# RWKV attention and a mixture of experts on one core: the combination of the experts' outputs moved from a stage of its own into the block loop

## The chip, the cores and the metric

The kernel runs on one core of a Trainium2 chip. The metric is the device time of one execution, in microseconds (us). A core has five engines with queues of their own: TensorE (PE), VectorE (DVE), ScalarE (ACT), GpSimd (POOL) and SyncE (SP). They are ordered only by semaphores, and each engine takes its own instructions in order, so an instruction that waits holds up everything queued behind it on that engine.

## The reference, cut to what matters

The input x is (2, 2048, 256), in float32. Two layers follow each other, each with a residual and a layer norm:

```python
x = layernorm(x + attn(x))     # RWKV: a scan over time, gates, projections
x = layernorm(x + ffn(x))      # mixture of 8 experts, the best 2 for each token

logits = x @ Wg + bg
scores, idx = top_k(logits, 2); scores = softmax(scores)
h = tokens @ W1[e] + b1[e]     # 256 -> 1024, for each expert e
a = gelu(h) for even e, silu(h) for odd e
y = a @ W2[e] + b2[e]          # 1024 -> 256
out = sum over the 2 chosen experts of score * y
```

There are 4096 tokens and so 8192 pairs of a token and an expert. The kernel computes y only for the chosen pairs.

## The kernel before

**Attention stage.** Eight chunks of 512 tokens (256 of each batch). `chunks(step)` writes the order of the work out by hand for each engine, as a software pipeline. In step i VectorE runs `stabilise(i)` (scans o_all, then nd), `divide(i-1)`, `place(i-3)`, `accumulate(i)` (b2v, two long scans), `numerator(i)`, `statistics(i-1)`, `choose(i-2)` and `lower_halves(i+2)`. ScalarE's step is `exponents(i)` (two Relu, two Exp, of which B is the first), `bonuses(i)`, a copy, `gates(i+1)` (Sigmoid), `upper_halves(i+2)` (which waits for TensorE's transposes xT), `inverse(i)` (Ln, Exp), `normalise_x1(i-1)` and the copies `copy_v(i+1)`. `accumulate` waits for the Exp of B, and TensorE makes the transposes of chunk i+2 in the order of its own step, behind the projection that waits for nd of chunk i. `choose` finds each token's two experts, `place` gives each pair a row in its expert's region of records_dram, and POOL's `send_records` scatters each token's row twice with indirect DMAs. A record is x1 (256 numbers), the pair's label and one slot number.

**Block stage.** The regions are cut into blocks of 256 rows with one expert each. At most 41 blocks can be used, here 35; the first two (`EARLY`, expert 0) run before the counts of all experts are known. A small table in SBUF holds each block's first row, expert and more. For each block t:

- ScalarE loads the records, `load_records(t+3)`, and runs `activate_block(t+1)`: for four groups b, two activations from hT_ps with bias (L1074) and a rounded copy aTh (L1080). A table load stands ahead of the first activation of a block.
- TensorE transposes the records of t+2, makes the first product of t+1 (hT_ps, L869) and the second of t (y_ps, L878, in two halves h). Each operand is held as an upper and a lower part, three products each.
- VectorE runs `outputs(t-1)` (y_sb = y_ps + bias, L1200), `halves(t+2)` and `lower_parts(t+1)` (aTl = hT_ps - aTh, L1192).
- POOL scatters y_sb to expert_out_dram, `scatter(t)`, two indirect DMAs a block (L670), and at the start of each expert splits the weights of the expert two ahead into upper and lower part, `split(e)` (L576, L580). SyncE loads those weights into one buffer, `raw`, once the split before is done.

Records live in 4 buffers (`RING`). The wait that releases the load of a block's records in ScalarE's `block_step` is on dest_done, which VectorE sets in `halves`, early:

```python
u = t + 3
if u.exists:
    with if_used(act, used, u):
        after(act, dest_done, (u - RING).upto(BH))
        load_records(u)
u = t + 1
if u.exists:
    with if_used(act, used, u):
        activate_block(u)
```

VectorE, ScalarE and POOL run the blocks 4 to 31 in hardware loops of four, TensorE all blocks in line. `if_used` puts a branch around blocks from 32 on.

**Combination stage.** When all scatters have landed (a wait of SyncE), 16 pieces of 128 tokens of each batch are taken: SyncE loads both outputs of each token (yy), VectorE adds score * first output to x1 (L1470), ScalarE scales the second (L1122), VectorE adds it (L1478) and makes statistics (L1484, L1492), POOL makes rstd (L686 to L691), ScalarE normalises (L1135), SyncE stores.

## Time and profile before

| | us |
|---|---|
| median of 3 runs (lowest, highest) | 736.69 (736.32, 737.68) |
| the profiled execution, its own time | 733.24 |
| its span, from the first to the last instruction | 731.5 |
| TensorE busy | 636.5 (87%) |
| VectorE busy | 457.7 (63%) |
| ScalarE busy | 392.8 (54%) |
| POOL busy | 304.9 (42%) |
| TensorE's granted clock, mean | 0.922 of full |

Busy times are of the one profiled execution. The instructions of an engine are named by line, operation and the program's tile names with buffer numbers left out; an arrow and a name in brackets behind a row is what ended the idle time before it. Busy time of PE is modelled from pipelined matmuls. Instructions that load a register, branch or wait are not counted as busy; they appear with a q behind the engine's name.

### The profile page before, as it was taken

The numbers are of one execution on the slowest core, as the hardware profiler recorded it, in microseconds if no ns is written. First come the engines' busy times: TensorE is split into PE (matmuls) and PEld (weight loads), VectorE is DVE, ScalarE is ACT, GpSimd is POOL, SyncE is SP. The second block draws the span as 40 slices with busy tenths as digits, with TensorE's granted clock in tenths as the row PEclk, the third lists the DMA queues.
The fourth block names the chain that finished last, engine by engine and source line by source line (L and its number), as shares of the span: only waits on it lengthen the run. The fifth ranks groups of instructions, "written<-read, shape, count | busy, mean of one in ns | idle before, by whom it ended". The sixth has DMA issues, their size and how long they took to land.

```text
span 731.5 us, 14706 instructions
## 1 busy us (share of the span) xinstructions
PE 636.5 (87%) x4472; PEld 595.0 (81%) x4472; DVE 457.7 (63%) x963; ACT 392.8 (54%) x715; POOL 304.9 (42%) x353
## 2 busy tenths in 40 slices
PE   5999999999957599999999999999999999997000
PEld 4887878878746499999999999999999999996000
DVE  3769999999994575574554654455444444432694
ACT  3566586577651263645545464655636364542474
POOL 5111044644655557282371641551921722122363
PEclk9999999999975599999999999999999999999555
DMA  8400232322226436905142141141141112101893
GB/s 254 137 29 1 87 101 82 107 91 83 88 87 231 144 101 223 330 28 175 44 136 70 44 160 52 42 161 46 49 154 38 39 46 59 32 27 32 276 304 117
DMA packets 57116, 78.75 MB, mean 108 GB/s; under 512 B 5190, under 2 KB 46611, under 8 KB 56884
## 3 DMA queue, kind: packets, MB, share of 16 engines
q1 hardware_dynamic: 41540, 51.59, 21.8%
q0 software_dynamic: 6496, 16.99, 6.5%
q10 hardware_dynamic: 8976, 8.72, 4.3%
q8 instruction: 73, 1.20, 0.7%
q14 instruction: 31, 0.25, 0.1%
HBM read 49.14 MB, written 28.92 MB: 107 GB/s over the span
## 4 chain that ended last, share of the span: by engine, by line
PE 67%; DVE 16%; issue 7%; ACT 3%; POOL 2%; DMA 2%; SPq 0%; ACTq 0%; DVEq 0%; POOLq 0%
PE hT_ps L869 27%; PE y_ps L878 26%; PE vr_ps L722 4%; PE k_ps L722 4%; PE xT_ps L887 2%; PE wo_ps L730 2%; DVE o_all L1214 2%; PE small_ps L744 1%; DVE stats L1312 1%; DVE newton L1237 1%; DVE newton L1235 1%; DVE newton L1242 1%; POOL rstd_c L689 1%; DVE num L1304 1%; DVE num L1307 1%
## 5 line engine op out<-in xcount | busy, mean ns | idle before, releaser
L869 PE MATMUL hT_ps<-xTh,wx 128*128 128x256 f32 x1120 | 211.3, 287 | 0.7 <-issue 0.6
L878 PE MATMUL y_ps<-wx,aTh 128*128 128x256 f32 x1088 | 197.5, 283 | 0.9 <-DVE y_sb L1200 0.9
L869 PEld LDWEIGHTS hT_ps<-xTh,wx 128*128 128x128 f32 x1120 | 178.2, 193 | 1.0 <-issue 0.9
L878 PEld LDWEIGHTS y_ps<-wx,aTh 128*128 128x128 f32 x1088 | 169.7, 192 | 1.1 <-issue 1.1
L1192 DVE TENSOR_TENSOR aTl<-hT_ps,aTh 128x512 fp32r<-128x512 f32 x140 | 93.1, 688 | 119.2 <-ACT aTh L1080 119.2
L670 POOL DMA_INDIRECT expert_out_dram<-y_sb,dest x70 | 68.3, 976 | 238.0 <-DVE y_sb L1200 222.3
L869 PE MATMUL hT_ps<-xTl,wx 128*128 128x256 f32 x560 | 159.2, 284 | 0.0
L878 PE MATMUL y_ps<-wx,aTl 128*128 128x256 f32 x544 | 154.0, 283 | 0.0
L1074 ACT ACT_TABLE_LOAD x33 | 42.3, 1283 | 170.4 <-PE hT_ps L869 165.2
L1074 ACT ACTIVATE hT_ps<-hT_ps,b_c 128x256 f32<-128x256 f32 x280 | 113.8, 469 | 18.2 <-DVE dest L1182 14.8
L869 PEld LDWEIGHTS hT_ps<-xTl,wx 128*128 128x128 f32 x560 | 108.3, 193 | 0.0
L878 PEld LDWEIGHTS y_ps<-wx,aTl 128*128 128x128 f32 x544 | 104.4, 192 | 0.0
L635 POOL DMA_INDIRECT records_dram<-rec,slot_i x64 | 75.2, 1175 | 63.4 <-DVE rec L1338 33.9
L722 PE MATMUL vr_ps<-xh,wq 128*128 128x512 f32 x256 | 87.5, 414 | 0.0
L1080 ACT ACTIVATE aTh<-hT_ps 128x512 fp32r<-128x512 f32 x140 | 84.2, 647 | 0.0
L1200 DVE TENSOR_TENSOR y_sb<-y_ps,b_b 128x256 f32<-128x256 f32 x70 | 29.3, 424 | 79.6 <-PE y_ps L878 77.7
L580 POOL TENSOR_TENSOR wx<-staging,wx 128x512 fp32r<-128x512 f32 x56 | 70.4, 1300 | 0.6
L722 PEld LDWEIGHTS vr_ps<-xh,wq 128*128 128x128 f32 x256 | 50.3, 196 | 11.7
L722 PE MATMUL vr_ps<-xl,wq 128*128 128x512 f32 x128 | 52.1, 407 | 0.0
L722 PE MATMUL k_ps<-xh,wq 128*128 128x512 f32 x128 | 44.1, 417 | 4.4 <-DVE nd L1221 2.3
L730 PE MATMUL wo_ps<-wo,newton 128*128 128x256 f32 x128 | 36.4, 435 | 7.5 <-DVE newton L1242 3.8
L730 PEld LDWEIGHTS wo_ps<-wo,newton 128*128 128x128 f32 x128 | 27.4, 217 | 13.1 <-issue 4.2
(194 smaller groups left out, 855.2 us busy)
## 6 DMA issues: line engine op xcount, KB each, us to landing
staging<-in_L_ffn_W SPq DMA_DIRECT2D x16, 1024.0 KB, 8.5
recs<-records_dram ACTq DMA_DIRECT2D x33, 258.0 KB, 2.7
yy<-expert_out_dram SPq DMA_DIRECT2D x16, 512.0 KB, 5.5
xin<-in_L_attn_x SPq DMA_DIRECT2D x16, 256.0 KB, 4.3
xres<-in_L_attn_x SPq DMA_DIRECT2D x16, 256.0 KB, 3.0
x_dram<-rec SPq DMA_DIRECT2D x16, 256.0 KB, 3.4
xx<-x_dram SPq DMA_DIRECT2D x2, 2048.0 KB, 20.2
out<-res SPq DMA_DIRECT2D x16, 256.0 KB, 3.7
```

The lines of the kernel that those rows point to most:

```text
L580: pool.tensor_tensor(wx[:, e % 2, 1, at], raw[:, at], wx[:, e % 2, 0, at].bitcast(F32), ALU.subtract).then_inc(weights_ready if n == LOWER ...
L635: pool.indirect_dma_start(xs, bass.IndirectOffsetOnAxis(ap=slot_i[at][:, n:n + 1], axis=0), rec[at][:, j, :], None, bounds_check=DUMMY - 1 ...
L670: pool.indirect_dma_start(ys, bass.IndirectOffsetOnAxis(ap=dest[t.slot][:, h:h + 1], axis=0), y_sb[t.slot][:, h, :], None, bounds_check=2 ...
L722: ins = pe.matmul(out_ps.rearrange("p (b t) -> p b t", b=B), wq[:, mat, now, part, cc, oc * P:(oc + 1) * P], xpart[c.slot][:, cc, :, now:n ...
L730: ins = pe.matmul(wo_ps[:, h, :], mixed[:, cc, b, h * P:(h + 1) * P], wo[:, cc, :], start=cc == 0, stop=cc == CC - 1)
L869: ins = pe.matmul(hT_ps[b][:, f, :], wx[:, s, part, off:off + P], xpart[t.slot % 2][:, cc, :], start=k == 0, stop=k == len(terms) - 1)
L878: ins = pe.matmul(y_ps[h], apart[t.slot % 2][:, fc, h * P:(h + 1) * P], wx[:, s, part, off:off + C], start=k == 0, stop=k == len(terms) - 1)
L887: ins = pe.transpose(xT2_ps[:, cc, h * P:(h + 1) * P], recs[u.slot][:, h, cc * P:(cc + 1) * P], ident[:])
L1074: act.activation(hT_ps[b][:, f, :], hT_ps[b][:, f, :], func, bias=b1_c[:, bass.ds(expert * FC + (2 * b + f), 1)]).then_inc(act_done, 1)
L1080: act.activation(aTh[u.slot % 2][:, 2 * b - 2:2 * b, :], hT_ps[b - 1][:], ACT.Copy).then_inc(aTh_done, 1)
L1192: dve.tensor_tensor(aTl[u.slot % 2][:, 2 * b:2 * b + 2, :], hT_ps[b][:], aTh[u.slot % 2][:, 2 * b:2 * b + 2, :].bitcast(F32), ALU.subtract ...
L1200: dve.tensor_tensor(y_sb[u.slot][:, h, :], y_ps[h], b2_b[:, bass.ds(expert * C, C)], ALU.add).then_inc(y_done, 1)
```

## The change

The combination stage is gone. A record has five numbers beside x1 instead of two: the token, the slot of its best expert, the larger of its two slots, and its two weights. VectorE's `mark` finds for each row of a block whether its token's other share is still to come or already there. Two times weight * (y + b2) is added to x1, which makes a *share*; the two shares of a token add up to twice the row before the layer norm (hence 4 * EPS). The first share of a token is scattered over its row of x1_dram (`keep_shares`); the block with the second share gathers the first (`gather`), adds, makes statistics, normalises and scatters the finished rows to the output (`send_rows`). The weights are split by ScalarE (upper part) and VectorE (lower part) in four pieces each, at the first block of the expert before. ScalarE loads records for t+4 at the end of its step and waits for the shares of t ahead of it. All engines run the blocks in line. The scores are two Sigmoids of ScalarE in the attention stage (`weigh`). The diff, cut to its core:

```diff
+            def weigh(c):
+
+                at = c.number % RECS
+                act.wait_ge(gap_done, c.upto(1))
+                scattered(act, c)
+                act.activation(rec[at][:, :, C + 3], gap[:], ACT.Sigmoid, scale=-1.0).then_inc(weighed, 1)
+                act.activation(rec[at][:, :, C + 4], gap[:], ACT.Sigmoid).then_inc(weighed, 1)
...
+                if (i - 3).exists and i.number < NCH:
+                    weigh(i - 3)
                 if i.exists:
...
                     inverse(i)
+                if i.number == NCH:
+                    weigh(i - 2)
                 if (i - 1).exists:
                     normalise_x1(i - 1)
+                if i.number in (NCH - 1, NCH + 1):
+                    weigh(i - 2)
...
+            rows_1 = x1d.rearrange("b t c -> (b t) c")
+            rows_2 = out.rearrange("b t c -> (b t) c")
+
+            def spread_z(t):
+                pool.wait_ge(mv_z_done, since_second(t) * BH)
+                after(pool, row_done, since_second(t - RING) * BH)
+                pool.tensor_tensor(var_z[:], mv_z[t.slot][:, :, 1], eps4_b[:], ALU.add).then_inc(var_done, 1)
+                pool.wait_ge(var_done, since_second(t))
+                pool.tensor_tensor(rstd_z[t.slot][:], var_z[:], half_neg[:, 0:BH], ALU.pow).then_inc(rstd_z_done, 1)
+
+            def keep_shares(t):
+
+                pool.wait_ge(marks, t.upto(8))
+                pool.wait_ge(share_done, t.upto(BH))
+                take_wait(pool)
+                for h in range(BH):
+                    pool.indirect_dma_start(
+                        rows_1, bass.IndirectOffsetOnAxis(ap=where_to[t.number % MARKS][:, 0, h:h + 1], axis=0),
+                        share[t.slot][:, h, :], None, bounds_check=TOKENS - 1, oob_is_err=False).then_inc(share_out[t.slot], 16)
+
+            def gather(t):
+
+                pool.wait_ge(marks, t.upto(8))
+                pool.wait_ge(share_out[(t - 1).slot], (t - 1).turn(16 * BH, 16 * BH))
+                after(pool, sum_done, since_second(t - RING))
+                take_wait(pool)
+                for h in range(BH):
+                    pool.indirect_dma_start(
+                        other[t.slot][:, h, :], None, rows_1,
+                        bass.IndirectOffsetOnAxis(ap=where_to[t.number % MARKS][:, 1, h:h + 1], axis=0),
+                        bounds_check=TOKENS - 1, oob_is_err=False).then_inc(other_in[t.slot], 16)
+
+            def send_rows(t):
+                pool.wait_ge(row_done, since_second(t) * BH)
+                take_wait(pool)
+                for h in range(BH):
+                    pool.indirect_dma_start(
+                        rows_2, bass.IndirectOffsetOnAxis(ap=where_to[t.number % MARKS][:, 1, h:h + 1], axis=0),
+                        row_out[t.slot][:, h, :], None, bounds_check=TOKENS - 1, oob_is_err=False).then_inc(out_done[t.slot], 16)
+
+            keep_shares(early_block(0))
+
+            def block_step(t):
+                for stage, u in ((keep_shares, t - 1), (send_rows, t - 2), (gather, t), (spread_z, t - 1)):
+                    if stage is keep_shares:
+
+                        if t.exists:
+                            with if_used(pool, used, t, t.number - 1):
+                                stage(u)
+                    elif u.exists and with_second(u):
+                        with if_used(pool, used, u, t.number - 1):
+                            stage(u)
+
+            blocks_in_line(pool, used, 2, block_step)
...
+                slot = pe.value_load(par_t[0:1, bass.ds(t.number, 1)], min_val=0, max_val=1)
+                full = pe.value_load(full_t[0:1, bass.ds(t.number, 1)], min_val=0, max_val=1)
+                pe.wait_ge(aTl_done, t.upto(FC // 2))
+                pe.wait_ge(share_done, (t - 1).upto(BH, 1))
+                with pe.If(slot == 0):
+                    product2(t, 0, 0)
+                with pe.Else():
+                    product2(t, 1, 0)
+                pe.wait_ge(share_done, (t - 1).upto(BH))
...
+            def split_upper(t):
+
+
+                kind = act.value_load(split_t[0:1, bass.ds(t.number, 1)], min_val=0, max_val=2)
+                with act.If(kind > 0):
+                    expert = act.value_load(next_t[0:1, bass.ds(t.number, 1)], min_val=0, max_val=E - 1)
+                    slot = act.value_load(opp_t[0:1, bass.ds(t.number, 1)], min_val=0, max_val=1)
+                    for h in range(BH):
+                        act.wait_ge(mm2_done[h], (t - 1).upto(1))
...
+                    act.wait_ge(raw_in, expert * 32 + 64)
+                    take_wait(act)
+                    for n in range(SPLITS):
+                        at = bass.ds(n * WE // SPLITS, WE // SPLITS)
+                        act.activation(wx[:, bass.ds(slot, 1), 0, at].rearrange("p a b -> p (a b)"), raw[:, at], ACT.Copy).then_inc(hi_done, 1)
...
-            act.wait_ge(dest_done, early_block(0).upto(BH))
+            act.wait_ge(share_done, early_block(0).upto(BH))
             load_records(early_block(4))
             activate_block(early_block(2))
+            act.wait_ge(share_done, early_block(1).upto(BH))
+            load_records(early_block(5))
             used = blocks_in_use(act)
 
             def block_step(t):
-                u = t + 3
-                if u.exists:
-                    with if_used(act, used, u):
-                        after(act, dest_done, (u - RING).upto(BH))
-                        load_records(u)
                 u = t + 1
                 if u.exists:
                     with if_used(act, used, u):
                         activate_block(u)
...
+                if t.number == EARLY:
+                    act.wait_ge(split_known, 1)
+                split_upper(t)
+                u = t + RING
+                if u.exists:
+                    with if_used(act, used, u):
+                        act.wait_ge(share_done, t.upto(BH))
+                        load_records(u)
+
+            blocks_in_line(act, used, 0, block_step)
...
+            def mark(u, own):
+
+
+                n = u.slot % 2
+                rows = recs[u.slot]
+                dve.tensor_tensor(is_top[n][:], rows[:, :, C + 1], own, ALU.is_equal).then_inc(marks, 1)
+                dve.tensor_tensor(is_late[n][:], rows[:, :, C + 2], own, ALU.is_equal).then_inc(marks, 1)
+                dve.tensor_tensor(is_early[n][:], rows[:, :, C + 2], own, ALU.not_equal).then_inc(marks, 1)
+                dve.tensor_tensor(lead[n][:], rows[:, :, C + 3], rows[:, :, C + 4], ALU.subtract).then_inc(marks, 1)
...
+                dve.wait_ge(marks, u.upto(8, 2))
+                dve.scalar_tensor_tensor(out=where_to[u.number % MARKS][:, 0, :], in0=is_late[n][:], scalar=float(NOWHERE),
+                                         in1=rows[:, :, C], op0=ALU.mult, op1=ALU.add).then_inc(marks, 1)
+                dve.wait_ge(marks, u.upto(8, 3))
+                dve.scalar_tensor_tensor(out=where_to[u.number % MARKS][:, 1, :], in0=is_early[n][:], scalar=float(NOWHERE),
+                                         in1=rows[:, :, C], op0=ALU.mult, op1=ALU.add).then_inc(marks, 1)
+                dve.wait_ge(marks, u.upto(8, 4))
+                dve.scalar_tensor_tensor(out=twice[n][:], in0=is_top[n][:], scalar=2.0, in1=lead[n][:],
+                                         op0=ALU.mult, op1=ALU.mult).then_inc(marks, 1)
+                dve.wait_ge(marks, u.upto(8, 7))
+                dve.scalar_tensor_tensor(out=weight[u.slot][:], in0=rows[:, :, C + 4], scalar=2.0, in1=twice[n][:],
+                                         op0=ALU.mult, op1=ALU.add).then_inc(marks, 1)
...
+            def share_half(u, h, expert):
+
+                if h == 0:
+                    after(dve, share_out[u.slot], u.turn(16 * BH))
+                    after(dve, sum_done, since_second(u - RING))
+                    dve.wait_ge(marks, u.upto(8))
+                dve.wait_ge(mm2_done[h], u.upto(1))
+                dve.tensor_tensor(y_ps[h], y_ps[h], b2_b[:, bass.ds(expert * C, C)], ALU.add).then_inc(y_done, 1)
+                dve.wait_ge(y_done, u.upto(BH, h + 1))
+                dve.scalar_tensor_tensor(out=share[u.slot][:, h, :], in0=y_ps[h], scalar=weight[u.slot][:, h:h + 1],
+                                         in1=recs[u.slot][:, h, 0:C], op0=ALU.mult, op1=ALU.add).then_inc(share_done, 1)
+
+            def shares(u):
+                expert = dve.value_load(ex_t[0:1, bass.ds(u.number, 1)], min_val=0, max_val=E - 1)
                 for h in range(BH):
-                    dve.wait_ge(mm2_done[h], u.upto(1))
-                    dve.tensor_tensor(y_sb[u.slot][:, h, :], y_ps[h], b2_b[:, bass.ds(expert * C, C)],
-                                      ALU.add).then_inc(y_done, 1)
+                    share_half(u, h, expert)
+
+            def add_other(u):
+                dve.wait_ge(other_in[u.slot], in_ring(u) * 16 * BH)
+                after(dve, out_done[u.slot], (in_ring(u) - 1) * 16 * BH)
+                dve.wait_ge(share_done, u.upto(BH))
+                dve.tensor_tensor(row_out[u.slot][:], share[u.slot][:], other[u.slot][:], ALU.add).then_inc(sum_done, 1)
+                dve.wait_ge(sum_done, since_second(u))
+                for h in range(BH):
+                    dve.bn_stats(stats_z[u.slot][:, h, :], row_out[u.slot][:, h, :]).then_inc(bn_z, 1)
+                dve.wait_ge(bn_z, since_second(u) * BH)
+                take_wait(dve)
+                for h in range(BH):
+                    dve.bn_aggr(mv_z[u.slot][:, h, :], stats_z[u.slot][:, h, :]).then_inc(mv_z_done, 1)
+
+            def normalise(u):
+                dve.wait_ge(rstd_z_done, since_second(u))
+                for h in range(BH):
+                    dve.tensor_scalar(row_out[u.slot][:, h, :], row_out[u.slot][:, h, :], mv_z[u.slot][:, h, 0:1],
+                                      rstd_z[u.slot][:, h:h + 1], ALU.subtract, ALU.mult).then_inc(row_done, 1)
...
+                kind = dve.value_load(split_t[0:1, bass.ds(t.number, 1)], min_val=0, max_val=2)
+                with dve.If(kind > 0):
+                    expert = dve.value_load(next_t[0:1, bass.ds(t.number, 1)], min_val=0, max_val=E - 1)
+                    slot = dve.value_load(opp_t[0:1, bass.ds(t.number, 1)], min_val=0, max_val=1)
...
+                        dve.wait_ge(hi_done, expert * SPLITS + (n + 1))
+                        take_wait(dve)
+                        flat = lambda part: wx[:, bass.ds(slot, 1), part, at].rearrange("p a b -> p (a b)")
+                        dve.tensor_tensor(flat(1), raw[:, at], flat(0).bitcast(F32),
+                                          ALU.subtract).then_inc(weights_ready if n == SPLITS - 1 else lower_done, 1)
...
+                u = t - 1
+                if u.exists and with_second(u):
+                    with if_used(dve, used, u, known):
+                        add_other(u)
+                if t.exists:
+                    with if_used(dve, used, t, known):
+                        shares(t)
+                        if t.number == EARLY:
+                            split_steps()
+                            dve.wait_ge(split_known, 1)
+                        split_lower(t)
+
+            blocks_in_line(dve, used, 2, block_step)
```

`split_steps` is twelve small operations on VectorE (up to 128x246), each waiting for the one before, that fill the tables split_t, next_t and opp_t; ScalarE waits for them once, at t = 2.

## Rows read from the trace of the kernel before

**Rows 1.** The page's part 4, the chain that ended last, shares of the span by line.

```profile
PE hT_ps L869 27%; PE y_ps L878 26%; PE vr_ps L722 4%; PE k_ps L722 4%; PE xT_ps L887 2%; PE wo_ps L730 2%; DVE o_all L1214 2%; PE small_ps L744 1%; DVE stats L1312 1%; DVE newton L1237 1%; DVE newton L1235 1%; DVE newton L1242 1%; POOL rstd_c L689 1%; DVE num L1304 1%; DVE num L1307 1%
```

**Rows 2.** Windows: start:end, length; busy us (x instructions) by engine, PEclk, DMA share, GB/s.

```profile
95.00:120.00 25.00, 24.59 (x121) 20.27 (x120) 24.27 (x56) 16.70 (x24) 13.17 (x15) 0.93 0.32 107
300.00:400.00 100.00, 100.00 (x839) 100.00 (x838) 54.78 (x85) 52.12 (x107) 44.96 (x36) 1.00 0.36 117
680.00:690.00 10.00, 0.00 (x0) 0.00 (x0) 7.59 (x22) 4.75 (x11) 3.46 (x8) 0.50 0.92 323
```

**Rows 3.** VectorE's timeline, end of the block stage: start us, length us, instruction [idle before].

```profile
672.41 0.42 DVE L1200 TENSOR_TENSOR y_sb<-y_ps,b_b 128x256 f32<-128x256 f32 x1 [2.27 <-PE y_ps L878]
```

**Rows 4.** The chain in order of time, block stage: start us, us, what.

```profile
300.88 5.75 PE hT_ps L869 x48
...
312.82 5.75 PE hT_ps L869 x48
```

**Rows 5.** ScalarE's timeline, block stage.

```profile
292.10 1.28 ACT L1074 ACT_TABLE_LOAD   x1 [1.61 <-PE hT_ps L869]
...
314.36 1.28 ACT L1074 ACT_TABLE_LOAD   x1 [5.66 <-PE hT_ps L869]
```

**Rows 6.** ScalarE's timeline, attention stage.

```profile
91.19 0.21 ACT L1008 ACTIVATE xh<-xh 128x4 fp32r<-128x4 f32 x1 [4.27 <-PE xT_ps L713]
...
92.39 1.28 ACT L1017 ACT_TABLE_LOAD   x1
...
94.77 1.28 ACT L1019 ACT_TABLE_LOAD   x1
...
101.85 1.05 ACT L981 ACTIVATE B<-B 128x1024 f32<-128x1024 f32 x1
...
116.91 0.21 ACT L1008 ACTIVATE xh<-xh 128x4 fp32r<-128x4 f32 x1 [4.75 <-PE xT_ps L713]
...
202.87 1.05 ACT L981 ACTIVATE B<-B 128x1024 f32<-128x1024 f32 x1
```

**Rows 7.** VectorE's timeline, attention stage.

```profile
96.47 1.38 DVE L1221 SCALAR_TENSOR_TENSOR nd<-o_all,consts_c,k_ps 128x512 f32<-128x512 f32 x2
...
102.93 1.23 DVE L1276 TENSOR_TENSOR b2v<-B,v 128x1024 f32<-128x1024 f32 x1
...
204.99 1.22 DVE L1276 TENSOR_TENSOR b2v<-B,v 128x1024 f32<-128x1024 f32 x1
```

**Rows 8.** VectorE's groups by line: instruction, xcount | busy us, mean ns | idle before.

```profile
L1470 DVE SCALAR_TENSOR_TENSOR zz<-yy,score,xx 128x256 f32<-128x256 f32 x32 | 13.7, 468 | 9.1 <-DMA yy<-expert_out_dram 9.0
L1484 DVE BATCH_NORM_STATS2 stats_c<-zz 128x6 f32<-128x256 f32 x32 | 11.9, 411 | 0.0
...
L1478 DVE TENSOR_TENSOR zz<-zz,y 128x512 f32<-128x512 f32 x16 | 10.9, 682 | 3.8 <-ACT y L1122 3.7
...
L1304 DVE TENSOR_TENSOR num<-bonus,p_all 128x1024 f32<-128x1024 f32 x8 | 9.9, 1233 | 0.3
...
L1492 DVE BATCH_NORM_AGGREGATE mv_c<-stats_c 128x2 f32<-128x6 f32 x32 | 3.9, 161 | 0.2 <-DVE stats_c L1484 0.2
```

**Rows 9.** ScalarE's queue at L1065, 289 to 293 us: xcount: ns, first to last start.

```profile
L1065 ACTq TENSOR_LOAD <-row_t x1: 282/282/282, 290.2 to 290.2; - x1
```

**Rows 10.** VectorE's timeline, block stage.

```profile
297.92 1.29 DVE L1192 TENSOR_TENSOR aTl<-hT_ps,aTh 128x512 fp32r<-128x512 f32 x2 [0.52 <-ACT aTh L1080]
```

**Rows 11.** VectorE's queue at L1448: xcount: ns min/median/max, first to last start.

```profile
L1448 DVEq TENSOR_LOAD <-ex_t x34: 300/305/319, 291.4 to 666.0; - x34
```

**Rows 12.** POOL's groups by line, columns as in rows 8.

```profile
L670 POOL DMA_INDIRECT expert_out_dram<-y_sb,dest x70 | 68.3, 976 | 238.0 <-DVE y_sb L1200 222.3 <-issue 14.9
...
L689 POOL TENSOR_TENSOR rstd_c<-var_e,half_neg 128x2 f32<-128x2 f32 x16 | 11.1, 696 | 1.3
```

**Rows 13.** DMA issues: xcount, median us from issue to landing.

```profile
expert_out_dram<-y_sb,dest POOLq DMA_INDIRECT x70, 2.9
```

**Rows 14.** POOL's timeline, attention stage.

```profile
209.51 1.88 POOL L635 DMA_INDIRECT records_dram<-rec,slot_i  x1 [0.30 <-issue]
```

383 lines of the change are left out of this document (142 added, 241 removed).

## The prediction

> **What bounds the kernel now.** I read the page's chain of waits first: two lines of TensorE, hT_ps (27%) and y_ps (26%), make half of it [rows 1]. The windows then show three stages. Up to about 255 us runs the attention stage, where VectorE is busy 24.3 of 25 us. From there to 672.8 us runs the block stage, with TensorE busy 100 of 100 us, VectorE only 55 and ScalarE 52. Behind 672.8 us TensorE does nothing (0.00 us): the combination takes 731.5 - 672.8 = 58.7 us of the span [rows 2, 3]. The chain in order of time gives the period of a block: 312.82 - 300.88 = 11.94 us, which is two products of 5.75 us and four transposes [rows 4]. 35 blocks are used, two of them early. ScalarE idles 5.66 us in each period until TensorE's first product is there [rows 5]. So the question is not whether the 58.7 us can go, but whether the block stage stays at 11.94 us when the combination's work is laid into it. S(t) below is the moment when both shares of block t are done.
>
> **The attention stage: +8.0.** Each chunk gets two Sigmoids on 128x4 in `weigh`, ahead of `exponents`, for chunks 3 to 7. ScalarE's table then has to go from Exp to Sigmoid and back: two loads of 1.28 and about 0.25 for the two small operations, 2.8 us. (Bounds for one chunk: 0 if both loads fell into idle time, 1.5 if Sigmoid's table also had Exp; no gain is possible, nothing is taken out of ScalarE's chain.) Is it hidden? ScalarE starts when the transposes xT are there (91.19) and runs without idle to the end of B's Exp at 101.85 + 1.05 = 102.90; VectorE starts b2v at 102.93 [rows 6, 7]. No slack at all: chunk 3 pays 2.8. Chunk 4 pays nothing more, because ScalarE's start at 116.91 hangs on TensorE's transposes, which follow nd of chunk 3 (done at 97.85) by 19 us, and that has not moved; chunk 5 pays 2.8 again, 6 nothing. In chunk 7 B is ready at 203.92 and b2v starts at 204.99: 1.1 of slack, 1.7 paid. Sum 7.3. One more operation of 128x4 in `place` adds some 0.09 to the full VectorE in 8 chunks: 0.7. The scores' three steps go from the table (1 us), but VectorE waits for ScalarE behind them, so nothing is gained.
>
> A rule of the Trainium skill (ScalarE: Activation LUTs, "What ACT_TABLE_LOAD costs") puts a switch of tables at 1.28 us of load and a drain of 1.38, 2.66 together. The trace does not show the drain: the load at 92.39 ends at 93.67 and the next load row (94.77) follows one operation of 1.06 without a gap [rows 6]. With the rule a chunk would pay 5.6 and the stage 5.6 + 5.6 + 4.5 + 0.7 = 16.4.
>
> **Into the block stage: +0.4.** The split of expert 1's weights leaves POOL; ScalarE's four copies (about 1 us each) lie in time in which it waits for the pad rows. VectorE gets four subtractions of 128x1024 at 1.23 [rows 8] between `halves` of blocks 2 and 3, and the marks; by its sum (four times 1.16, two halves of 1.4, two marks of 1.1, shares of 1.8) its first lower part of block 2 is done some 0.4 after TensorE wants it. Expert 1's weights stay in time. POOL's clearing of `other`, the records' 12 more bytes a row, and the longer unrolled code cost nothing by this: nobody waits for them early. Their cost if that is wrong: a microsecond or two, once.
>
> **The block stage: a new loop.** TensorE's own waits are harmless: share_done(t-1) is asked for behind a first product of 5.75 us. What matters is `block_step` of ScalarE. It ran `load_records(t+3)` on dest_done, a mark long set. Now it waits for share_done(t), and only behind that come load_records(t+4) and then activate_block(t+2), queued on the same engine. VectorE's step t+1 does lower_parts(t+2), which need those activations, then add_other(t), then shares(t+1). So S(t) releases ScalarE, ScalarE releases VectorE, and VectorE makes S(t+1): a loop of one block in which TensorE has no part. Its length:
> - ScalarE from the wait to its table load: the load of the row number starts at 290.2, the table load at 292.10 with the DMA issue and the expert's number between them; with the semaphore 2.0 [rows 5, 9].
> - Table load to the end of VectorE's last lower part: 297.92 + 1.29 - 292.10 = 7.1 [rows 5, 10].
> - add_other: 128x512 addition 0.69, two statistics 0.74, a wait of 0.16, two aggregates of which the second starts 0.08 later: 1.75 [rows 8].
> - the expert's number behind it: the load alone is 0.31 [rows 11], with the register work that follows it 0.65, as ScalarE's is 0.5 out of its 2.0. It may be hidden (0) or cost 1.0 with the branches; now VectorE reads it while a long operation still runs, here the one ahead is 0.16 long, so I take it whole.
> - two halves of shares: addition 0.42 [rows 3], the multiply-add 0.47 [rows 8], the second half overlapping a little: 1.65 to 1.8, taken 1.65.
>
> Sum 2.0 + 7.1 + 1.75 + 0.65 + 1.65 = 13.15 us, against 11.94. Bounds: 12.1 with every doubtful term at its least, 14.0 at its most. Marks (eight small operations), halves and `normalise` lie in VectorE's wait for the activations.
>
> **The sum.** S(2) is 301.8: the product ends near 300.9, plus 0.9. `split_steps` (12 small operations; 1.9 at 0.16 each, 5.6 at 0.47, taken 3.7) come next, and ScalarE waits for them: 305.5. Then 0.6 for the split's kind, 2.0, 7.1 and 1.75 give S(3) = 317.0. From there to S(30) are 27 turns: 355.0. Six of them hold a split of weights. ScalarE's four copies end just as the share comes; VectorE's part, four times 1.16 and the numbers it reads, pushes its next lower parts behind the activations by about 2.5 (0 if it caught up, 5 if nothing overlapped): 15. S(30) = 687.0. From t = 31 ScalarE's wait lies in a branch not taken (block t+4 is unused), and TensorE and VectorE finish the last four blocks in turn: with S(30) as zero, S(31) is 13.15, the product of block 32 starts on the first share at 12.3 and ends at 18.1, the first product of 34 at 24.2, the product of 33 at 30.0; its share lets the last product start at 30.4, and S(34) is 37.1. S(34) = 724.1, where now it is 672.8.
>
> **The tail: 58.7 becomes 16.** The combination's stage goes whole: SyncE's wait for all scatters, the loads back, 32 sums, the statistics, POOL's and ScalarE's part, the stores. What comes in its place is each block's own, and only the last two blocks' stand behind the end. Behind S(34): POOL sends block 32's rows, gathers, spreads block 33, then 34 in turn; an indirect DMA is 0.98 with 0.30 before it, the power 0.69, the last landing 2.9 [rows 12, 13]. keep 3.2, send 2.6, gather 2.6, its landing and the addition 4.5, spread, normalise and send 34: end 16 behind S(34), 13 to 20 with the branches.
>
> Span: 724.1 + 16 + 8.0 = 748.1, that is +16.6 on 731.5 (the 0.4 is in S(2)). The profiled execution took 733.24 us with 1.74 around its span, so it would read 749.8. The median of the runs is 736.69; +16.6 gives 753.3.
>
> **Rivals.**
> - *TensorE stays the bound (faster).* If the loop is no longer than 11.94, S(34) stays at 672 and the end is 672 + 0.4 + 16 + 8.0 = 696.8, time 702. For it: VectorE's and ScalarE's busy sums are far under the period, and the value loads may hide. Against: the chain is serial, and its largest parts (7.1, 2.0) stand in the trace whole. Between 11.94 and 13.15 it goes by 27 us for each microsecond; no change is at a loop of 12.5.
> - *POOL becomes the bound (slower still).* Six indirect DMAs a block instead of two. At 1.28 each it has 7.7 of 13.15. But a row of before shows 1.88 with 0.30 ahead of it, while VectorE ran a long scan [rows 14]. Six at 2.18 and a spread of 1.2 are 14.3: 1.1 more a block, some 31 us, 784. It decides from 2.0 each. The Trainium skill (SBUF — State Buffer, the box on the "DVE blocks DMA" trap) says that GpSimd can't write descriptors while VectorE holds the shared port; the change gives VectorE more such operations. The slow row agrees with it, but most of the 70 rows at 976 ns ran beside VectorE too.
> - *The attention stage pays nothing*: -8.0, 745; against it stands the slack of 0.03 us.
> - *The table's drain exists*, as a mechanism of the five chunks: +8.4, 762. The gapless rows speak against.
> - That the change doesn't do what it says: the records are loaded four blocks ahead in name, but released later than now in time. This is the forecast itself.
>
> **How the numbers follow.** Forecast 0.60 (its own range 735 to 772); a short loop, 702 to 735, 0.22; POOL 0.07; attention free 0.06; drain 0.05. A measurement of this kernel can tell 0.2% (1.5 us) from no change. Faster 0.22, within 0.2% 0.02, slower 0.76. The loop's bounds of 12.1 and 14.0 give 725 and 776; with the other terms I take 720 to 778.
>
> **What would show it.** In the changed profile: ScalarE's idle time ahead of its table load or row load released by VectorE's shares, not by TensorE; a period near 13.15 between first products; TensorE idle about 1.2 us a block in two gaps; the first table load behind copy_v in chunks 3 to 7 and a wait of b2v for B. A period of 11.94 with idle ScalarE would make the forecast wrong, and so would shares that end long before ScalarE asks.

## The result: 774.5 us, 5.0% slower

The changed kernel takes 774.47 us (median of 4 runs, 773.57 to 776.31) beside 737.18 us for the kernel before: a ratio of 1.050 [1.049, 1.052]. The forecast was 753.3: slower, and the time lies in the outer range of 720 to 778, but above the 735 to 772 of the main case; +16.6 us stood where +37.3 were measured. The profiled execution took 776.31 us, its span is 774.4 (731.5 before). The two profiled executions lie 42.9 us apart in span and the medians 37.3, because the one of before was 3.9 us under its median and this one 1.8 over; the stages below add up to the 42.9.

The page's parts on the chain and the clock. PEclk is TensorE's granted clock in tenths, in 40 slices:

```profile
PEclk9999999999855699998999998999999999899995
DVE 31%; PE 23%; issue 19%; ACT 12%; ACTq 5%; DVEq 3%; another core or an unknown queue 1%; DMA 1%; POOL 1%; SPq 1%; POOLq 0%
```

Before, two lines of TensorE alone made half of the chain [rows 1]. Now VectorE leads it, and ScalarE, VectorE and their register loads (ACTq, DVEq) make half. Two windows of [rows 2] again. Columns: window, its length, busy us of PE, PEld, DVE, ACT, POOL, then PEclk, DMA share and GB/s. TensorE is no longer full in the block stage, and its clock is under 1.00 there:

```profile
95.00:120.00 25.00, 23.80 (x123) 19.27 (x122) 21.42 (x44) 18.99 (x28) 11.49 (x13) 1.00 0.33 107
300.00:400.00 100.00, 93.49 (x760) 91.61 (x759) 65.55 (x177) 53.72 (x105) 38.59 (x42) 0.97 0.26 80
```

One turn of the loop, VectorE's side. Columns: start, duration, engine and line, in brackets the idle time before and its releaser:

```profile
487.69 0.42 DVE L1210 TENSOR_TENSOR y_ps<-y_ps,b_b 128x256 f32<-128x256 f32 x1
488.14 0.48 DVE L1212 SCALAR_TENSOR_TENSOR share<-y_ps,weight,recs 128x256 f32<-128x256 f32 x1
...
494.11 0.69 DVE L1195 TENSOR_TENSOR aTl<-hT_ps,aTh 128x512 fp32r<-128x512 f32 x1 [2.13 <-ACT aTh L1063]
...
496.53 1.29 DVE L1195 TENSOR_TENSOR aTl<-hT_ps,aTh 128x512 fp32r<-128x512 f32 x2 [0.52 <-ACT aTh L1063]
497.74 0.68 DVE L1224 TENSOR_TENSOR row_out<-share,other 128x512 f32<-128x512 f32 x1
498.45 0.75 DVE L1227 BATCH_NORM_STATS2 stats_z<-row_out 128x6 f32<-128x256 f32 x2
499.34 0.25 DVE L1231 BATCH_NORM_AGGREGATE mv_z<-stats_z 128x2 f32<-128x6 f32 x2
500.30 0.43 DVE L1210 TENSOR_TENSOR y_ps<-y_ps,b_b 128x256 f32<-128x256 f32 x1 [0.71 <-issue]
...
501.63 0.48 DVE L1212 SCALAR_TENSOR_TENSOR share<-y_ps,weight,recs 128x256 f32<-128x256 f32 x1
```

And ScalarE's side of the same turn, its record load and then its table load:

```profile
489.34 0.39 ACTq L1049 DMA_DIRECT2D recs<-records_dram  x1
490.62 1.28 ACT L1057 ACT_TABLE_LOAD   x1 [7.24 <-issue]
```

The shares of block 14 end at 488.62. ScalarE, idle for 7.24 us with nothing of TensorE to wait for (it idled 5.66 for TensorE in [rows 5]), asks for the records 0.72 later and loads its table at 490.62. The chain in order of time goes there too, from the share to ScalarE's load of the row number (L1048):

```profile
488.14 0.49 DVE share L1212
488.66 0.28 ACTq L1048
```

VectorE's last lower part ends at 497.82, add_other at 499.59, the row of the number takes 0.71, and the shares of block 15 end at 502.11. 2.00 + 7.20 + 1.77 + 0.71 + 1.81 = 13.49 us, forecast as 2.0 + 7.1 + 1.75 + 0.65 + 1.65 = 13.15. It is the loop that was forecast, and it sets the period: the turns without a split take 13.39 to 13.77 us.

Where the 42.9 us of span came from. S(t) is again the end of both shares of block t, read from the rows of L1212:

| stretch | forecast | after | difference |
|---|---|---|---|
| up to S(2) | 309.8 (301.8 + 8.0) | 316.9 | +7.1 |
| S(2) to S(3), with split_steps | 15.2 | 15.5 | +0.3 |
| S(3) to S(30), 27 turns, 6 with a split | 370.0 | 379.3 | +9.3 |
| S(30) to S(34) | 37.1 | 43.9 | +6.8 |
| S(34) to the end of the span | 16 | 18.9 | +2.9 |
| span (the rows are rounded) | 748.1 | 774.4 | +26.3 |

### The profile page after: what moved, and what is told of

It reads as the page before. It is cut to its first block, busy times and chain, and to the rows that moved or that the text cites. A ratio compares the mean times of both kernels' runs of the same rounds, so it can differ in the third digit from the quotient of the medians.

```text
span 774.4 us, 14695 instructions
## 1 busy us (share of the span) xinstructions
PE 657.0 (85%) x4472; PEld 604.4 (78%) x4472; DVE 552.1 (71%) x1398; ACT 411.8 (53%) x709; POOL 349.1 (45%) x422
## 4 chain that ended last, share of the span: by engine, by line
DVE 31%; PE 23%; issue 19%; ACT 12%; ACTq 5%; DVEq 3%; another core or an unknown queue 1%; DMA 1%; POOL 1%; SPq 1%; POOLq 0%
DVE aTl L1195 6%; ACT hT_ps L1057 5%; PE vr_ps L697 5%; PE hT_ps L844 5%; PE k_ps L697 4%; PE y_ps L853 3%; DVE share L1212 3%; DVE y_ps L1210 3%; DVE stats_z L1227 3%; DVE wx L1514 2%; ACT aTh L1063 2%; PE wo_ps L705 2%; DVE row_out L1224 2%; PE small_ps L719 2%; ACTq L1049 1%
## 5 line engine op out<-in xcount | busy, mean ns | idle before, releaser
L844 PE MATMUL hT_ps<-xTh,wx 128*128 128x256 f32 x1120 | 224.4, 298 | 16.2 <-DVE aTl L1195 15.5
L844 PEld LDWEIGHTS hT_ps<-xTh,wx 128*128 128x128 f32 x1120 | 188.6, 204 | 21.9 <-DVE aTl L1195 20.8
L853 PEld LDWEIGHTS y_ps<-wx,aTh 128*128 128x128 f32 x1088 | 167.0, 189 | 17.5 <-issue 17.5
L844 PE MATMUL hT_ps<-xTl,wx 128*128 128x256 f32 x560 | 165.1, 295 | 0.0
L1057 ACT ACTIVATE hT_ps<-hT_ps,b_c 128x256 f32<-128x256 f32 x280 | 113.4, 468 | 22.2 <-PE hT_ps L844 15.6
L631 POOL DMA_INDIRECT x_dram<-share,where_to x68 | 72.9, 1072 | 104.9 <-issue 96.1
L844 PEld LDWEIGHTS hT_ps<-xTl,wx 128*128 128x128 f32 x560 | 114.4, 204 | 0.0
L590 POOL DMA_INDIRECT records_dram<-rec,slot_i x64 | 76.5, 1196 | 65.7 <-DVE rec L1375 34.9
L651 POOL DMA_INDIRECT out<-row_out,where_to x64 | 62.8, 981 | 75.6 <-DVE row_out L1236 53.3
L642 POOL DMA_INDIRECT other<-x_dram,where_to x64 | 65.9, 1030 | 25.0 <-issue 24.7
L1210 DVE TENSOR_TENSOR y_ps<-y_ps,b_b 128x256 f32<-128x256 f32 x70 | 29.9, 428 | 28.3 <-issue 22.4
```

What stands on the lines that cost most here:

```text
L590: pool.indirect_dma_start(xs, bass.IndirectOffsetOnAxis(ap=slot_i[at][:, n:n + 1], axis=0), rec[at][:, j, :], None, bounds_check=DUMMY - 1 ...
L631: pool.indirect_dma_start(rows_1, bass.IndirectOffsetOnAxis(ap=where_to[t.number % MARKS][:, 0, h:h + 1], axis=0), share[t.slot][:, h, :], ...
L642: pool.indirect_dma_start(other[t.slot][:, h, :], None, rows_1, bass.IndirectOffsetOnAxis(ap=where_to[t.number % MARKS][:, 1, h:h + 1], ax ...
L651: pool.indirect_dma_start(rows_2, bass.IndirectOffsetOnAxis(ap=where_to[t.number % MARKS][:, 1, h:h + 1], axis=0), row_out[t.slot][:, h, : ...
L844: ins = pe.matmul(hT_ps[b][:, f, :], wx[:, s, part, off:off + P], xpart[t.slot % 2][:, cc, :], start=k == 0, stop=k == len(terms) - 1)
L853: ins = pe.matmul(y_ps[h], apart[t.slot % 2][:, fc, h * P:(h + 1) * P], wx[:, s, part, off:off + C], start=k == 0, stop=k == len(terms) - 1)
```

## Experiments

Ratios are to the kernel before on the same chip; the changed kernel's is 1.050. Where a stage is meant and not the whole, S(2) and S(3) to S(30) of the profiled execution stand beside the time, because chips and executions differ in the early part by more than some effects do.

**The two orders.** First, add_other behind the shares, everything else as in the change:

```
-   add_other(t - 1)
    shares(t)
+   add_other(t - 1)
    split_lower(t)
```

> Only VectorE's order in a step changes: add_other(t-1) behind shares(t). The records are still loaded four ahead behind share(t). Theory of the loop: 1.77 us of it go, and a part of the 0.71 us of the number read, which now lies behind a longer operation; 11.2 to 11.7 is under TensorE's 11.94, so 27 turns give back 42 us, and the end some 3 to 7 more because the last product waits less for VectorE: 725 to 732 us if the splits keep their 2.45 us, 715 if they hide. Rival (the sum of VectorE's work, which is unchanged, sets the period): no change.

718.04 us, ratio 0.981 [0.979, 0.984]. Most turns take 11.04 to 11.42 in place of 13.5 (three early ones up to 11.9), S(3) to S(30) 328.3 in place of 379.3: 51.0 us. The sum of VectorE's work is the same in both, so the rival falls. What the order takes out of the loop is add_other, 1.77, and the number read, 0.71: 13.49 - 2.48 = 11.01. In the profiled run the shares of blocks 14 and 15 end at 460.63 and 471.77, and add_other now starts behind them:

```profile
460.15 0.48 DVE L1212 SCALAR_TENSOR_TENSOR share<-y_ps,weight,recs 128x256 f32<-128x256 f32 x1
460.56 0.68 DVE L1224 TENSOR_TENSOR row_out<-share,other 128x512 f32<-128x512 f32 x1
...
471.29 0.48 DVE L1212 SCALAR_TENSOR_TENSOR share<-y_ps,weight,recs 128x256 f32<-128x256 f32 x1
```

Expected were 725 to 732 us if the splits keep their cost; the kernel before is 4.7 us faster on this chip too (732.52). The split turns stayed at 15.3 to 15.4: their distance to a plain turn is 4.3 now, 2.4 before. The slower loop had hidden a part of them. With the splits the mean turn is 12.16 us: the shares catch up behind a split at the length of the shorter loop, and over a whole group TensorE, with 11.73 of work a block, is close to the limit.

**Lengthening the loop, in either order.** The two statistics of add_other are taken twice, the first time into a spare tile:

```
+   for h in range(BH):
+       dve.bn_stats(spare[:, h, :], row_out[u.slot][:, h, :]).then_inc(spare_done, 1)
    for h in range(BH):
        dve.bn_stats(stats_z[u.slot][:, h, :], row_out[u.slot][:, h, :]).then_inc(bn_z, 1)
```

> add_other takes its two statistics a second time into a spare tile: 0.75 us more on VectorE between the last lower part and the share. Theory of the loop: every turn is 0.75 us longer, 31 turns, +23 us: 797.5 us, period 14.25. Rival (another engine sets the period and VectorE has slack, 5 of 13.5 us idle): no change, 774.5.

> The doubled statistics (0.75 us a block on VectorE) in the kernel with add_other behind the shares. Theory: they lie beside ScalarE's 2.0 us and first activations, not in the loop: 0 to 3 us more than g1_behind_again, all in the split turns, against 16 us where add_other stands ahead of the shares. Rival (VectorE's sum of work counts in either order): 16 to 23 us more.

In the changed order: 785.49 us, ratio 1.072 [1.070, 1.074], plain turns 14.05 to 14.53, S(3) to S(30) 398.2, which is +18.9 or 0.70 a turn. (The whole time is 11 us over the changed kernel's and not the 23 that were expected, mainly because S(2) is 308.3 here and 316.9 there.) With add_other behind the shares: 748.48 us, S(3) to S(30) 346.6 against 345.2 in the run beside it, +1.4. The same operations cost 19 us in one order and 1.4 in the other. That settles the loop. (In whole times it is less plain, 5.2 us in the second pair, where 0 to 3 were expected; but the runs of the two overlap, 740.46 to 749.54 and 743.23 to 750.66.)

**POOL's control.** POOL's power of a block is taken twice, again into a spare tile.

> A control for the doubled statistics: POOL takes its power of a block a second time into a spare tile, 0.73 us more a block on POOL. Theory (the loop ScalarE to VectorE sets the changed kernel's block stage, POOL has 4 us of idle a turn): no change from the changed kernel, ratio 1.050 to 1.052. Rival (POOL with its six DMAs and the power sets the period): 31 x 0.73 = +23 us, ratio 1.081.

773.80 us, ratio 1.047 [1.045, 1.050]; S(3) to S(30) 379.5 against 379.3. POOL does not set the period; that rival is out.

**Cutting the loop at ScalarE.** Loads only three blocks ahead need no fresh share:

```
-   act.wait_ge(share_done, early_block(1).upto(BH))    # ahead of the loop
-   load_records(early_block(5))
    ...
-   u = t + RING
+   u = t + RING - 1
    ...
-   act.wait_ge(share_done, t.upto(BH))
+   act.wait_ge(share_done, (t - 1).upto(BH))
    load_records(u)
```

> ScalarE loads a block's records three blocks ahead, behind the share of the block before (long done), so it no longer waits for share(t) ahead of its activations. Theory (the loop S(t) to ScalarE to VectorE to S(t+1), 13.49 us a turn, sets the block stage): the loop is cut, the period falls to TensorE's 11.94, 27 turns give back 27 x 1.55 = 42 us, and up to 15 more if the six splits hide: 717 to 733 us in place of 774.5. Rival (VectorE's or POOL's own sum of work sets the period): no change, 770 or more.

A miss: 782.05 us, ratio 1.069 [1.067, 1.071], slower than the change. The period did fall, to 12.35 to 12.9 in twelve of the 21 turns without a split, but S(3) to S(30) is 382.3 and S(2) to S(3) alone 23.5. TensorE's waits (engine, line, waited for: us in all, times, longest) name the new one:

```profile
PE xT_ps L862 <- DMA recs<-records_dram: 44.6, 21, 9.4
```

The load stands at the end of ScalarE's step, behind the activations, and is one block less ahead, so the transposes wait for it. I had costed the wait that goes and not asked what is late next. Two repairs, one with the depth of the change and one with three ahead:

```
POOL, behind keep_shares(t - 1), which waits for share(t - 1) anyway:
+   load_records(t - 1 + RING)        # as a DMA of POOL; ScalarE's wait and load go
```

> The record loads from block 4 on go to POOL's queue, behind keep_shares, which waits for share(t) anyway; they stay four ahead. ScalarE then waits for no share, and VectorE's order is the changed kernel's. Theory of the loop (cut at ScalarE, loads early enough, unlike with the loads three ahead): turns of 11.7 to 11.94 outside the splits, 27 turns give 42 us back or more, 722 to 735 us. Rival (VectorE's own order, or POOL with a seventh DMA a block): turns of 13 us or more, 765 or more.

```
ScalarE, between the first and the second pair of activations of block t + 1:
+   act.wait_ge(share_done, (t - 1).upto(BH))
+   act.dma_start(recs[v.slot][:], ...)     # v = t + 3, its row number read ahead
```

> Loads three ahead as in e1_three_ahead, but issued by ScalarE between its first and second pair of activations, some 3.5 us earlier in its step. Theory (e1 lost what it won because TensorE's transposes waited 45 us in all for records that were asked for too late): that wait falls under 15 us, turns outside the splits 11.7 to 12.1, 725 to 740 us. Rival (ScalarE's share wait returns at the new place, or the loads' depth is not the cause): 765 or more.

726.53 us, ratio 0.984 [0.978, 0.989], and 721.45 us, 0.978 [0.976, 0.980]. S(3) to S(30) is 327.5 and 324.3. TensorE's wait for records, 44.6 us in all before the repair, is 2.6 in the second and a quarter in the first:

```profile
PE xT_ps L875 <- DMA recs<-records_dram: 11.7, 8, 3.9
```

So the loop cut at either of its two places gives 51 to 55 us of this stage back, if the records come in time.

**The split.** VectorE's four subtractions of a split shrink to 128x2; the lower halves of the weights of experts 2 to 7 are left out, ScalarE's part stays:

```
+   at = bass.ds(n * WE // SPLITS, 2)
    dve.tensor_tensor(flat(1), raw[:, at], flat(0).bitcast(F32), ALU.subtract)
```

> VectorE's four subtractions of 128x1024 in a split shrink to 128x2 (the lower halves of the weights of experts 2 to 7 are left out); ScalarE's table load and four copies stay. Theory (a split costs its turn 2.43 us because VectorE's 4.9 us of subtractions push its lower parts back): 6 x 2.43 = 14.6 us back, ratio 0.019 lower than the changed kernel's, every turn 13.5. Rival (the unforeseen table load and the copies on ScalarE are what a split costs): no change, split turns stay at 15.9.

762.05 us, ratio 1.034 [1.031, 1.037]; S(3) to S(30) 365.0, which is 14.3 less or 2.4 a split: the split turns became plain ones (13.42 to 13.55). ScalarE does load a table there that I had not seen coming (1.28 us, six times, ahead of its copies), but that costs nothing by itself. The rows of one split in the changed kernel:

```profile
455.11 1.28 ACT L1088 ACT_TABLE_LOAD   x1 [1.19 <-issue]
456.41 3.90 ACT L1088 ACTIVATE wx<-staging 128x1024 f32 x4
```

```profile
458.71 0.49 DVE L1212 SCALAR_TENSOR_TENSOR share<-y_ps,weight,recs 128x256 f32<-128x256 f32 x1
461.03 4.63 DVE L1514 TENSOR_TENSOR wx<-staging,wx 128x1024 f32 x4 [1.84 <-ACT wx L1088]
```

**The attention stage.** First, the Sigmoids moved to where their table is loaded, with POOL's spread put ahead of its sends:

```
ScalarE:  -   weigh(i - 3)      # ahead of exponents(i)
              gates(i + 1)
          +   weigh(i - 3)
POOL:     +   spread_of(i - 1)
              send_records(i - 3)
          -   spread_of(i - 1)
```

> The two Sigmoids of the scores move behind ScalarE's gates, where Sigmoid's table is loaded already, and POOL takes the spread of chunk i-1 ahead of the sends of chunk i-3. Theory (the attention stage pays the reload of Exp's table ahead of B's exponential in chunks 3, 5 and 7): 7 us back, 767.5 us, the first product of block 0 near 256 in place of 263.2. Rival (the delay comes from VectorE's added operations): 774.

773.28 us, ratio 1.055 [1.054, 1.057]: no gain. Chunk 7's `nd` starts at 202.59 (205.40 in the changed kernel; 203.9 to 205.0 in three runs on this chip with the Sigmoids ahead), so 1.3 to 2.8 us came back. But the sends of two chunks now stand ahead of the last chunk's spread, and ScalarE waits 17 us for it; the first product of block 0 starts at 268.66, in the three others at 258.2 to 258.8:

```profile
256.12 2.07 ACT L1006 ACTIVATE rec<-xres,shift,rstd 128x256 f32<-128x256 f32 x4 [17.26 <-POOL shift L569]
```

The run does not test the table loads alone. The next one comes nearer: no table load is left ahead of B's Exp, though POOL gets four small operations for it. The weights come without Sigmoid (the edit in short form):

```
ScalarE:  -   rec[..., C + 3] = Sigmoid(-gap);  rec[..., C + 4] = Sigmoid(gap)
          +   odds = Exp(gap)
POOL:     +   root = (1 + odds) ** -0.5;  rec[..., C + 3] = root * root
          +   rec[..., C + 4] = odds * rec[..., C + 3]
```

> The scores' weights without Sigmoid: ScalarE takes Exp of the gap (its table is loaded then), POOL adds one, takes the power and multiplies, in time in which it waits for VectorE's slots. Theory (two table loads ahead of B's exponential cost the attention stage 7.3 us): 7 us back, block 0's first product 7 us earlier than the changed kernel's. Rival (VectorE's added operations, or POOL as the new delay): 1 us or less.

761.29 us, ratio 1.034 [1.030, 1.038]: 13 us less than the changed kernel on that chip. Block 0's first product starts at 251.98, 9.9 us ahead of the changed kernel's 261.89 on the same chip, 7.1 of which are there at chunk 7 already (198.10 against 205.23); the rest is behind the last chunk. The 7 that were expected are those at chunk 7. The rest of the gain is no part of that theory. The profiled executions are 14.6 us apart at S(2) (301.2 against 315.8): 2.8 of them arise behind the last chunk and 4.7 in the first blocks, and no run separates their cause. VectorE's rows of chunk 7 in the two:

```profile
205.23 1.38 DVE L1257 SCALAR_TENSOR_TENSOR nd<-o_all,consts_c,k_ps 128x512 f32<-128x512 f32 x2
```

```profile
198.10 1.38 DVE L1265 SCALAR_TENSOR_TENSOR nd<-o_all,consts_c,k_ps 128x512 f32<-128x512 f32 x2
```

**The early part again.** The changed kernel once more:

> The changed kernel once more, unchanged, beside this chip's runs of the kernel before. If the 4.35 us in which ScalarE stood still in the early activations (no releaser shown) and the late start of the block stage belong to the kernel, they are there again and the ratio is 1.050; if they belong to that one chip, the first product of block 0 starts near 258.5, S(2) is near 308 as in the experiments so far, and the ratio is 1.040 to 1.045.

774.46 us, ratio 1.052 [1.047, 1.057]; S(2) is 315.8. So the late start is no accident of one chip. But the pause of 4.35 us is not there: at its place ScalarE waits 2.99 us for TensorE:

```profile
274.67 0.81 ACT L1057 ACTIVATE hT_ps<-hT_ps,b_c 128x256 f32<-128x256 f32 x2 [2.99 <-PE hT_ps L844]
```

And in three runs that shared another chip and whose early part is the change's, but for one record load in the first (loads three ahead, add_other behind, doubled statistics), the first product starts at 258.2 to 258.8 and S(2) is 307.6 to 308.8, also without the pause. The expectation's either-or was too coarse.

**Do the gains add?** One combination, and two with more in it:

> add_other behind shares and the weights by Exp, together, in the changed kernel. If the two work on different stages, their gains add: 51 us and 13 us against the changed kernel, ratio 0.964, about 711 us. If the first hid a part of the second, 718.

> f1 and the record loads on POOL's queue. The loop is then cut at both places, and what is left is VectorE's split: the turns with one stayed at 15.4 and 15.9 us in the two runs that cut the loop once, and average 12.1. Theory (the split's place in VectorE's order is the bound now): little more, 3 us or less against f1. Rival (ScalarE's wait for the share costs the split turns): 15 us.

> f2, and VectorE's part of a split moves behind halves and marks of the next step, so that TensorE's next first product no longer waits for it. Theory (TensorE waits for xTl behind the 5 to 6 us of the split): split turns fall from 15.9 to about 12 to 13, turns between are TensorE's 11.9, 6 to 12 us less than f2. Rival (the lower parts behind the split are what TensorE waits for): no change.

724.55, 729.79 and 730.69 us; ratios 0.983 [0.980, 0.986], 0.987 [0.984, 0.990], 0.989 [0.988, 0.991]. None did what its theory said: 711 (or 718), at most 3 us under the first, and 6 to 12 less than the second were expected. The third stayed with its rival, no change: the split turns are 15.4 to 15.9 as before. Exp's gain did not show against the first run with add_other behind, and neither the loads on POOL nor the split's new place helped. So the first two versions ran side by side:

> add_other behind shares once more, on the same chip as the next: ratio 0.981 to the kernel before, as on the first chip. If that chip was what made it look good, 0.985 to 0.99.

> The same with the weights by Exp. If the attention stage's gain (13 us in a run of its own) adds, 10 to 13 us less than g1_behind_again; if the block stage swallows it, because TensorE's idle time and low clock at the splits grow, within 3 us of it.

743.26 us, ratio 1.008 [1.005, 1.011], and 730.29 us, 0.992 [0.990, 0.995]. On one chip Exp gives its 13 us. What had misled me was the first run: the very kernel with ratio 0.981 there has 1.008 here. S(2) is 307.6 there and 319.3 here, S(3) to S(30) 328.3 and 345.2 (the profiled execution here, 748.32 us, is 5 over its median). The window 320:680 of both, here first, has the clock in its third column from the end:

```profile
320.00:680.00 360.00, 339.15 (x2768) 334.84 (x2767) 272.65 (x720) 206.29 (x394) 191.41 (x216) 0.97 0.26 79
```

```profile
320.00:680.00 360.00, 346.53 (x2897) 344.13 (x2896) 286.71 (x757) 218.41 (x420) 205.59 (x232) 0.99 0.27 82
```

In this order TensorE falls idle around the splits, and a stretch at its lower clock follows: behind five of six splits here, behind two there. 0.02 of the clock over 360 us is 7 of the 17 us between the two executions, and TensorE is idle 20.9 us here (360 - 339.15) and 13.5 there, another 7. Why the same order leaves it idle longer on one chip is open. With the loads between the activations the clock stays up:

> Loads between the activations and the weights by Exp together. In e11_loads_between TensorE's clock stays at its higher level through the splits, so nothing should swallow the attention stage's gain: ratio 0.978 - 0.018 = 0.960, about 708 us, S(3) to S(30) 324 us as in that run. If the gains do not add here either (as with add_other behind the shares, on one chip 13 us but from a worse block stage): 718 or more.

704.36 us, ratio 0.956 [0.953, 0.959]: the best version of all, 4.4% under the kernel before and 9% under the change. S(3) to S(30) is 322.2, and the gains of its two parts add, to a little more than their sum (0.960 expected):

```profile
320.00:680.00 360.00, 350.50 (x2946) 346.44 (x2945) 288.13 (x769) 218.67 (x419) 216.07 (x241) 1.00 0.27 84
```

TensorE is busy 350.5 of 360 us, at the full clock, with the combination laid into the stage. In the kernel before it is busy 350.5 of the 352 us from 320 to 672, and its 27 turns take 317.7 us: the combination now costs this stage 4.5 us. One more step on it:

```
    normalise(t - 2)
+   split_lower(t - 1)
    lower_parts(t + 1)
    ...
    shares(t)
-   split_lower(t)
```

> g3_between_exp, with VectorE's part of a split behind halves, marks and normalise of the next step. Theory (a split turn of 15.93 us holds 1.83 us in which VectorE waits for ScalarE's copies; that wait is then filled with 3 us of work that is ready): split turns 14.1, 6 x 1.8 = 8 to 11 us less than g3_between_exp. Rival (VectorE's sum over a group of blocks is at TensorE's limit, what a split turn gains the next turn loses): no change within 2 us.

741.98 us, ratio 1.005 [1.001, 1.009]: 38 us worse, against both expectations. Four split turns fell from 15.9 to 15.5 or 15.6, two stayed at 16.0 and 16.1, and plain turns, 10.1 to 11.4 before this edit, became 10.1 to 16.6. TensorE stands inside its products, with no releaser shown:

```profile
PE hT_ps L854 <- issue: 13.8, 29, 1.1
PE y_ps L863 <- issue: 9.1, 19, 1.0
```

In the run beside it these two make 3.6 us. That is 19 of the 38 us; ScalarE has idle time there too whose releaser the trace can't name, 21.9 us in eight places. Only VectorE's order differs between the two. Why TensorE, which waits for nothing there, should pause is open.

## Why the prediction was right in kind and wrong in size

- *The whole.* The mechanism, the loop, was right; the sum was 26.3 us short in span (about 5 of them lie between these executions and the medians). The steps that failed, by size: the loop's length (13.15, measured 13.49: 9.3 us), the last four blocks and the tail (37.1 + 16, measured 43.9 + 18.9: 9.7 us), and the way into the block stage (+0.4, measured +7.1 beyond it).
- *The bound.* The question was put rightly: not the 58.7 us at the end but the block stage. The loop S(t), ScalarE, VectorE, S(t+1) is there, part by part; three ways of cutting or stretching it show it.
- *Loop length, 13.15.* The period is 13.49. 0.34 us, from terms that were taken too short: shares 1.65 for 1.81 (the low end of the 1.65 to 1.8 that stand in the prediction), lower parts 7.1 for 7.20, number 0.65 for 0.71, add_other 1.75 for 1.77. 27 turns make 9.2 us of it. The step that failed in size is this one above all; "the second half overlapping a little" was a guess, and a term that is multiplied by 27 should not stand at its low end.
- *Splits, 15.* Right: 2.4 each, 14.3 by the run that takes VectorE's part away, and through VectorE, as argued. But ScalarE's copies do not end just as the share comes, as the prediction had it: a table load stands ahead of them that it had missed, and VectorE waits 1.84 us for them. That the 2.5 was right all the same is in part luck.
- *split_steps, 3.7.* 316.82 to 320.59: 3.8.
- *The attention stage, +8.0.* The first product of block 0 moved from 254.70 to 263.17, 8.5 us. The pattern is the forecast's too: against the kernel before, `nd` of chunks 3 to 7 starts at -0.4, +2.7, +3.6, +6.4 and +6.8 us, so chunks 3 and 5 pay some 3 us each and chunks 4 and 6 little. But in the three runs on the other chip the first product moved by 3.5 to 4.1 only, though `nd` of chunk 7 is 5.3 to 6.4 late there; what is made up behind the last chunk is not known. The rows of chunk 3 show the mechanism; compare [rows 6, 7], where B's Exp starts without a table load:

```profile
99.65 1.28 ACT L974 ACT_TABLE_LOAD   x1
100.95 0.21 ACT L974 ACTIVATE rec<-gap 128x4 f32<-128x4 f32 x1
101.06 0.19 ACT L975 ACTIVATE rec<-gap 128x4 f32<-128x4 f32 x1
101.16 1.05 ACT L950 ACTIVATE B<-nd 128x1024 f32<-128x1024 f32 x1
102.11 1.04 ACT L951 ACTIVATE A<-nd 128x1024 f32<-128x1024 f32 x1
103.16 1.28 ACT L953 ACT_TABLE_LOAD   x1
```

  Both loads are 1.28 us, and the row behind the first starts 0.02 after its end, so the drain (rival of 0.05) is not there. The rule of the Trainium skill (ScalarE: Activation LUTs, "What ACT_TABLE_LOAD costs") with 1.38 more does not hold for these loads.
- *Into the block stage, +0.4.* Another step that failed. In the profiled run +7.1 stand at S(2) beyond the 8.0. From the first product to S(2) it is 53.7 us, 46.2 in the kernel before. A pause of ScalarE in the activations of block 0 lies in that stretch:

```profile
275.98 0.81 ACT L1057 ACTIVATE hT_ps<-hT_ps,b_c 128x256 f32<-128x256 f32 x2 [4.35 <-remote]
```

  But the repeat of the changed kernel has no such pause and takes 53.9 us for the same stretch, so the pause alone does not explain it. In the three runs on the other chip the stretch is 49.0 to 50.1, and S(2), 307.6 to 308.8, is near the forecast's 309.8 by chance: the attention stage cost some 4 us less than forecast, the first blocks 2 to 3 more. I had written that the longer unrolled code costs nothing, "a microsecond or two, once" if that is wrong. What makes this stretch long stays open, and so does the pause. The Trainium skill (Runtime: NRT & Kernel Launch, "Instruction fetch mechanics") has instructions fetched block by block while the engine runs, which would allow such a pause. No row here ties it to a fetch.
- *The last four blocks, 37.1, and the tail, 16.* Measured 43.9 and 18.9, the third miss. The first product of block 34 ends where it was forecast, 24.2 behind S(30). Then VectorE does lower parts, add_other(32) and reads a number before it comes to the shares of block 33; I had let that share be ready with its product. TensorE waits 2.94 us, and then its clock drops:

```profile
744.93 0.50 PE L853 MATMUL y_ps<-wx,aTh 128*128 128x256 f32 x2 [2.94 <-issue]
```

```profile
745.00:750.00 5.00, 5.00 (x30) 5.00 (x31) 3.25 (x9) 0.00 (x0) 2.39 (x3) 0.66 0.10 28
750.00:760.00 10.00, 2.37 (x21) 2.17 (x19) 4.26 (x11) 0.00 (x0) 6.76 (x8) 0.84 0.18 54
760.00:774.00 14.00, 0.00 (x0) 0.00 (x0) 0.73 (x2) 0.00 (x0) 3.56 (x5) 0.50 0.10 32
```

  The clock costs the last product up to 3 us: S(33) to S(34) is 9.00 to 9.06 in this run, the repeat and the one with the small split, and 5.8 to 7.1 in four others with the same code there, whose last four blocks took 38.9 to 41.2; the mean clock from S(33) to S(34) is 0.84 in the three and 1.00 in the four. But the end does not hang on S(34). The chain at the end goes from the second share of block 33 through POOL, which stores that share, sends the finished rows of block 32 and gathers for block 34. S(34) (755.6) comes before the gathered rows have landed (757.7), so block 34 waits for POOL and not for TensorE:

```profile
746.09 0.49 DVE share L1212
...
748.88 2.09 DMA x_dram<-share,where_to
...
752.73 1.05 POOL other L642
...
755.40 0.74 POOL rstd_z L623
```

```profile
757.73 0.69 DVE L1224 TENSOR_TENSOR row_out<-share,other 128x512 f32<-128x512 f32 x1 [0.78 <-DMA other<-x_dram,where_to]
```

  From S(33) to the end of the span it is 27.6 to 29.1 us in all seven of these runs, whether S(34) comes early or late; the forecast has about 22. So the tail's 18.9, inside its 13 to 20, is luck: in the four others it is 21.7 to 23.0. The step that failed is S(33), at 34.9 behind S(30) where about 31 was forecast, and POOL's chain, which starts there and not at S(34). Of the 58.7 us of the combination 39.8 were won.
- *Rivals.* TensorE stays bound: it did not in the changed kernel. In the best version it nearly does (322.2 us for 27 turns, 317.7 before). Its 704 us beside the 702 of this rival is chance, since that 702 held 8.0 for the attention stage and 16 behind S(34), where this version has no such delay in its attention stage and 20.0 at the end. POOL: the doubled power refutes it, and its indirect DMAs of the block stage took 0.98 to 1.07 us in the mean, not the 1.88 of [rows 14]. Attention stage free: refuted by the 7.1 us that chunk 7 gained without Sigmoid.

## What to carry over

A load "farther ahead" whose wait stands in front of other work on its engine ties that work to the wait: ask of each new wait what is queued behind it, and walk the circle back to its releaser. The length of that circle, times the number of turns, is the price: 0.34 us in it were 9 here. When it is cut, ask what is late next (here the records). At the end of a pipeline ask which engine's chain is the last, here POOL's and not TensorE's. And judge by stages on one chip: the same kernel had ratios of 0.981 and 1.008 on two chips.
